# ScalarE's sixteen pairs of batches written out one by one, with one activation table load ahead of them

## The reference

```python
qh = (q @ Wq).reshape(B, N, NUM_HEADS, HEAD_DIM).transpose(0, 2, 1, 3)
kh = (kv @ Wk).reshape(B, M, NUM_HEADS, HEAD_DIM).transpose(0, 2, 1, 3)
vh = (kv @ Wv).reshape(B, M, NUM_HEADS, HEAD_DIM).transpose(0, 2, 1, 3)
scores = jnp.einsum('bhnd,bhmd->bhnm', qh, kh) * scale
attn = jax.nn.softmax(scores, axis=-1)
out = jnp.einsum('bhnm,bhmd->bhnd', attn, vh)
...
x = x + jnp.tanh(g_xattn[0]) * _L0_xattn_ref(_layernorm(x, axis=-1), ctx_512, ...)
x = x + jnp.tanh(g_ffn[0]) * _L0_ffn_ref(_layernorm(x, axis=-1), ...)
```

## Time and profile before

| | us |
|---|---|
| median of 3 runs | 1499.19 (1499.08 to 1499.24) |
| profiled execution, its own time | 1498.68 |
| its span, first to last instruction | 1497.0 |
| PE busy | 1441.7 |
| DVE busy | 1086.8 |
| ACT busy | 958.3 |
| one pair in the loop (first table load to the next) | 63.70 |

### The profile page before, as it was taken

How to read it: one execution, slowest core, us unless ns; L and a number is a source line. 1 busy time by engine, 2 the same in 40 slices (tenths; PEclk the granted TensorE clock), 3 DMA queues, 4 the chain that set the end, 5 groups by cost and what they waited for, 6 DMA issues and landing times.

```text
span 1497.0 us, 32793 instructions
## 1 busy us (share of the span) xinstructions
PE 1441.7 (96%) x9774; PEld 1344.9 (90%) x9774; DVE 1086.8 (73%) x2626; ACT 958.3 (64%) x2413; POOL 440.7 (29%) x676
## 2 busy tenths in 40 slices
PE   6999999999999999999999999998899999999998
PEld 6899999999999999999999999997689988888888
DVE  4778788887878878778787888878668634444448
ACT  4777777777777777777777776775363335455452
POOL 1013132331313313133231323324300135555520
PEclk9999999999999999999999999999999999999999
DMA  4011311212121130311213211141022256653235
GB/s 122 6 30 36 112 73 47 76 49 105 47 80 71 54 104 15 113 71 47 85 40 109 75 47 72 53 153 64 27 99 113 74 180 222 246 203 120 78 121 217
DMA packets 55294, 136.93 MB, mean 91 GB/s; under 512 B 10480, under 2 KB 38144, under 8 KB 51648
## 3 DMA queue, kind: packets, MB, share of 16 engines
q1 hardware_dynamic: 48608, 118.01, 22.7%
q0 software_dynamic: 6624, 18.13, 3.8%
HBM read 86.69 MB, written 49.43 MB: 91 GB/s over the span
## 4 chain that ended last, share of the span: by engine, by line
PE 78%; DVE 10%; issue 5%; ACT 5%; DMA 0%; ACTq 0%; DVEq 0%; POOL 0%; SPq 0%; POOLq 0%
PE bank L531 14%; PE bank L530 14%; PE bank L532 14%; PE bank L588 8%; PE bank L1590 6%; PE bank L933 5%; PE bank L925 5%; PE bank L1610 4%; DVE pT_lo L753 3%; PE bank L1614 2%; PE bank L1600 2%; DVE nmax L770 2%; ACT prob L678 1%; ACT L717 1%; ACT pT_hi L689 1%
## 5 line engine op out<-in xcount | busy, mean ns | idle before, releaser
L678 ACT ACTIVATE prob<-bank,nmax 128x375 f32<-128x375 f32 x448 | 258.7, 577 | 189.1 <-DVE nmax L770 187.2
L770 DVE TENSOR_REDUCE nmax<-bank 128x1 f32<-128x375 f32 x448 | 241.1, 538 | 48.4 <-PE bank L532 47.8
L753 DVE TENSOR_TENSOR pT_lo<-bank,pT_hi 125x384 fp32r<-125x384 f32 x448 | 246.0, 549 | 32.5 <-ACT pT_hi L689 30.7
L588 PE MATMUL bank<-keep_ident,prob 128*125 128x128 f32 x1344 | 225.4, 276 | 25.2 <-DVE pT_lo L753 22.9
L588 PEld LDWEIGHTS bank<-keep_ident,prob 128*125 128x125 f32 x1344 | 198.6, 187 | 45.8 <-DVE pT_lo L753 20.9
L689 ACT CAST pT_hi<-bank 125x384 fp32r<-125x384 f32 x448 | 212.6, 475 | 2.5 <-PE bank L588 2.4
L530 PE MATMUL bank<-attend_wvo_hi,zT_hi 128*112 128x256 f32 x512 | 169.5, 331 | 0.0
L530 PE MATMUL bank<-pT_hi,kv_hi 125*128 125x448 f32 x384 | 152.7, 398 | 6.1 <-DVE zT_lo L753 6.1
L530 PE MATMUL bank<-attend_kvT_hi,qp_hi 128*128 128x376 f32 x448 | 150.3, 335 | 0.2 <-DVE attend_kvT_lo L753 0.2
L531 PE MATMUL bank<-attend_kvT_hi,qp_lo 128*128 128x376 f32 x448 | 150.1, 335 | 0.0
L532 PE MATMUL bank<-attend_kvT_lo,qp_hi 128*128 128x376 f32 x448 | 149.0, 333 | 0.0
(11 more groups left out here) (234 smaller groups left out, 3729.3 us busy)
## 6 DMA issues: line engine op xcount, KB each, us to landing
w_split<-we_split SPq DMA_DIRECT2D x14, 2048.0 KB, 6.8
keep_weights<-w_split SPq DMA_DIRECT2D x14, 2048.0 KB
we_in<-in_w SPq DMA_DIRECT2D x28, 512.0 KB, 5.8
keep_y_all<-y_rows SPq DMA_DIRECT2D x14, 512.0 KB, 9.7
kv_in<-in_ctx SPq DMA_DIRECT2D x32, 187.5 KB
h_rows<-hrow SPq DMA_DIRECT2D x32, 112.4 KB, 2.1
keep_h_in<-h_rows SPq DMA_DIRECT2D x7, 514.0 KB, 8.3
x_in<-in_x SPq DMA_DIRECT2D x16, 224.0 KB, 2.8
```

The source lines that it names most:

```text
L588: last = nc.tensor.transpose(T[s % 2][0:MP, c * P:(c + 1) * P], prob[:, s % NB, c * MP:(c + 1) * MP], ident[:])
L678: nc.scalar.activation(prob[:, s % NB, :], score_bank(s)[:, 0:M], ACT.Exp, bias=nmax[:, s % NB:s % NB + 1], accum_out=psum_[:, s % NB:s % ...
L753: return nc.vector.tensor_tensor(dst, src, hi.bitcast(F32), ALU.subtract)
L770: nc.vector.tensor_reduce(nmax[:, s % NB:s % NB + 1], score_bank(s)[:, 0:M], AX, ALU.max, negate=True).then_inc(max_ready, 1)
```

## The change

ACT no longer calls `body_over_pairs`. Its body is written out for each of the 16 pairs, with numbers in place of registers, and the table load stands once ahead of all pairs instead of at the head of each. PE, DVE, POOL and SP keep their code and their loops. Lines behind the change have numbers one lower than before.

```diff
-            def body(p, jobs):
-                first = isinstance(p, int) and p == 0
-                nc.scalar.preload_act_table_set("natural_log_exp_and_others")
+            nc.scalar.preload_act_table_set("natural_log_exp_and_others")
+            for p in range(PAIRS):
+                first, jobs = p == 0, LAST if p == PAIRS - 1 else FULL
                 for s in range(STEPS):
                     if tile := back(p, s - 4, first):
                         turned(*tile)
...
                     for phase, q, b in second_norm(p, s, first):
                         if phase == "roots":
                             ln2_roots(2 * q + b)
-            body_over_pairs(act, body)
             last = PAIRS - 1
```

## The result

The changed kernel took 1487.1 us as the median of its comparable runs (1486.94, 1487.09 and 1489.15), the kernel before 1499.22: a ratio of 0.9925, 95% interval 0.9911 to 0.9939. One run of 1583.92 us, at a granted clock of 0.849, is left out. That is 12.1 us by the medians, where 11.8 were forecast.

What follows compares the result with a forecast made beforehand. PE was taken to bound the kernel, waiting on ACT's table load only at pair starts. Gains of 14 x 0.78 + 0.83 = 11.75 us took 1499.19 to 1487.4 us, range 1483.5 to 1492.5.

Steps and rivals of the forecast that it cites:

- What bounds the kernel, and the one place: Whole kernel: PE bounds it; ACT stands on PE's path only at each pair's start, in a wait of 1.18 us.
- at most 1.49 us a pair: Loop pair: it lasts 63.70 us with PE busy 62.21, so 1.49 us is the most winnable without removing a product.
- The load is paid in full, the loop costs nothing: ACT at pair starts: fifteen loads of 1.283 us go, 19.2 us of ACT's time; branch and register work cost nothing.
- DVE's maxima keep 0.4 us: Pair start: DVE's maxima stand ahead of `pT_lo`, so 0.36 to 0.44 us of PE's 1.18 us wait stays.
- the one by `pT_lo`: Pair start: gain sized by how soon `pT_lo` follows the maxima in mid-pair, 0.82 us a pair.
- The one by PE's transpose: Pair start: gain sized by how soon PE's transpose follows the maxima in mid-pair, 0.74 us a pair.
- The sum: Pair starts: 14 x 0.78 + 0.83 = 11.75 us gained, with 11.2 and 12.3 as ends.
- Nothing behind it is disturbed: Rest of each pair: the whole pair moves by 0.78 us, and the small waits further on stay.
- rival C: Later in the pair: DVE and POOL disturb each other, giving back 2.8 to 8.4 us, 1490.2 to 1495.8; chance 0.11.
- B: Pair starts: the whole 1.18 us wait comes back, 17.7 us in all, 1481.5 us; chance 0.09.
- D: Pair starts: no time gained, as a load still runs per pair or does not hold ACT, 1499.2; chance 0.03.
- E: ACT's longer list: fetching it, at most nine 16 KB packets, makes the kernel slower, 1505.4 us at 2.0 each; chance 0.03.

Runs made afterwards that it cites:

- both swaps and the roots first: Changed kernel with DVE's low part ahead of the maxima in steps 0 and 14, and ACT's two small roots ahead of the exps: 1473.6 us, ratio 0.9826.
- the kernel with step 0 swapped: Changed kernel with DVE's low part of the turned tile (`pT_lo`) ahead of the maxima in step 0 of each pair: 1480.29 us, ratio 0.9873.
- that with both: Changed kernel with DVE's low part ahead of the maxima in steps 0 and 14 of each pair, roots not moved: 1489.2 us, ratio 0.993.
- that with the roots first: Changed kernel with DVE's low part ahead of the maxima in step 0 only, and ACT's two small roots ahead of the exps: 1474.35 us, ratio 0.9829.

## Why the prediction was right

*What bounds the kernel, and the one place.* Right: the whole gain came at the pairs' starts, and PE's other work and waits in the pair stayed. Two readings beside it were too strong. "Almost all" of PE's waits being of that kind holds within the loop; over the whole kernel it is 22.9 of 47.7 us, and the longest single waits are two of 5.1 us elsewhere. And "at most 1.49 us a pair" took PE's busy time for a floor: with both swaps and the roots first a pair is 63.70 - 61.94 = 1.76 us shorter, with the same products, and PE is busy for 61.88 us of it in place of 62.21.

*The load is paid in full, the loop costs nothing.* Right, and shown by the loop with one load (62.88 us a pair) and the written-out pairs with a load each (63.70). One small thing was missed: without the load `pT_hi` starts 0.09 us after the start of the exps' last instruction, inside its 0.20 us; with the load it could not begin before that had ended. So `pT_hi` came 1.43 us earlier (157.91 - 156.39 - 0.09), not 1.30. DVE's maxima hid the difference.

*DVE's maxima keep 0.4 us.* Right, by the timeline of after and by the swap that then removed the rest. Of the two ways to size it, the one by `pT_lo` hit: 0.82 worked out, 0.83 measured. The one by PE's transpose (0.74) had borrowed the 0.69 us from `pT_lo`'s start to the transpose from the middle of the pair, but at the pair's start the transpose kept its 0.60.

*The sum.* 11.75 forecast with 11.2 and 12.3 as ends. The trace gives 14 x 0.83 + 0.83 = 12.4 for the pairs' starts. Against that stand a wait of 0.3 us in pair 15, below, and the spread of runs; the medians give 12.1. For the profiled execution 1486.9 us had been forecast, and it took 1489.15; nearly all of the difference is the 2.1 us at its start.

*Nothing behind it is disturbed.* Right in pairs 1 to 14. In pair 15, PE waits once for DVE where it had not:

```profile
PE bank L530 <- DVE x L813: 0.3, 1, 0.3
```

Ahead of it stands a scaling of `prob` on DVE, beside an instruction of POOL. These two in the kernel before, in the kernel after, and in the second profile of the kernel after:

```profile
1012.50 0.60 DVE L779 TENSOR_SCALAR prob<-prob,prob_inv 128x375 f32<-128x375 f32 x1
1010.05 2.85 POOL L1037 TENSOR_SCALAR keep_w_in<-keep_w_in,keep_tanh_g 128x1024 f32<-128x1024 f32 x1
```

```profile
1002.30 0.92 DVE L778 TENSOR_SCALAR prob<-prob,prob_inv 128x375 f32<-128x375 f32 x1
1000.16 2.84 POOL L1036 TENSOR_SCALAR keep_w_in<-keep_w_in,keep_tanh_g 128x1024 f32<-128x1024 f32 x1
```

```profile
1000.53 1.25 DVE L778 TENSOR_SCALAR prob<-prob,prob_inv 128x375 f32<-128x375 f32 x1
998.73 2.84 POOL L1036 TENSOR_SCALAR keep_w_in<-keep_w_in,keep_tanh_g 128x1024 f32<-128x1024 f32 x1
```

POOL's instruction ends 0.40, 0.70 and 1.04 us after the scaling has begun, the scaling ends some 0.2 us behind it each time, and PE waits 0, 0.3 and 0.6 us. This is the mechanism of rival C, and against it the forecast had held that POOL's work begins from an event of the same pair. In pair 15 it does not: this run of POOL's work begins when a transfer of weights lands (POOL waits 5.08, 5.25 and 5.65 us for it), and so its place differs even between two executions of one kernel. That the change brought the wait is not shown: the written-out pairs with a load in each, as slow as before, have it too (0.2 us), and the loop with one load has not (a scaling of 0.59 us).

*The rivals.* B, the whole 1.18 us, did not come since DVE was next, as argued. D fell with the first profile. E fell with the written-out kernels: the trace after shows just the added 0.15 MB, and even PE's list at full length left no wait for a fetch. The nine packets of the forecast took q8's 16 KB for the queue of ACT's list; q14's packets were of 8 KB before too (0.22 MB in 27), so twice as many came, and the price per packet that decides E was half the one worked out. The Trainium skill's "Instruction fetch mechanics" ("Runtime: NRT & Kernel Launch"), by which straight code is fetched ahead in 16 KiB blocks and mostly hidden, agrees in the block's size with q8, the queue of PE's list (1.36 MB in 83 packets with all lists written out, 16.4 KB each), but not with q14, which carried ACT's longer list (0.37 MB in 45 packets, 8.2 KB each). Its warning of a stall is for a taken branch that leaves the fetched window. ACT's loop took nothing for its branch, but it is too short to test the warning: from the counts, 1,164 rows for 13 more bodies and 856 instructions fewer executed in 14 turns, a turn is an estimated 155 rows, some 20 KB at the 0.15 MB for 1,164 rows, which fits in the two such blocks that the same section gives as the window.

## What to carry to other kernels

Look for the cost of an instruction at its place, not in its total: fifteen table loads were worth 12 us at the head of a pair and nothing where the engine idled. Before you price the removal of a wait, read what the engine that gave it does next in its own list; the gain ends there, and the same sequence elsewhere in the trace, without the wait, gives its size. And when a reordering that should gain loses, look for a helper engine whose long instruction has moved onto one of the engine that counts: here the start of POOL's work was worth more than the wait that was being removed.

## What was not expected of the hardware

- Two table loads that switch between sets took 1.28 us each, with 0.01 us between them and 0.02 behind; a reload of the active set took the same 1.28. The further 1380 ns of drain that the Trainium skill ("ScalarE: Activation LUTs", "What ACT_TABLE_LOAD costs") adds for a switch is not seen.
- Behind waits of 2.48 us PE's granted clock fell in 5 of 15 pairs, to 0.79 to 0.81 over the 8 us behind the wait, at some 1.5 us each; behind 1.18 us waits in none of pairs 1 to 14.
- A DVE scaling in SBUF of 128x375, 0.42 us by itself, lasted up to 2.63 us in the loop and ended some 0.2 us behind the end of POOL's first subtraction, in the kernel with step 0 swapped, in that with both, and in that with the roots first. The DVE instructions next to it that read PSUM kept their 0.5 to 0.6 us.
- The same thing makes PE's longest wait of the attention, and it stands in pair 15 of the kernel before and of the kernel after alike (5.07 and 5.09 us); no experiment here goes for it. In the kernel before the scaling ends 0.2 us behind the second of two subtractions of POOL:

```profile
1024.42 5.37 DVE L779 TENSOR_SCALAR prob<-prob,prob_inv 128x375 f32<-128x375 f32 x1
1027.24 2.34 POOL L1046 TENSOR_TENSOR keep_w2s_lo<-keep_w_in,keep_w2s_hi 128x1024 fp32r<-128x1024 f32 x1
1030.47 0.71 PE L530 MATMUL bank<-pT_hi,kv_hi 125*128 125x448 f32 x1 [5.07 <-DVE zT_lo L753]
```

Over the 10 us from this product on PE's granted clock is 0.78, and 0.79 at the same place in the kernel after.
